# The causal mask moved from TensorE to VectorE in a fused Perceiver block

## What is computed

```python
x = x + fake_quant(layernorm(x)) @ fake_quant(ctx)          # cross step, 16 x 1024 x 1024 context
h = layernorm(x)
q, k, v = split(h @ qkv_w + qkv_b)                          # 32 heads of 32
q, k = rope(q), rope(k)
scores = einsum("bqhd,bkhd->bhqk", q, k) / sqrt(32)
scores = scores + (1.0 - causal) * -66504.0                 # keys after the query are hidden
x = x + (softmax(scores) @ v) @ out_w + out_b
x = x + layernorm(x) @ W.T + bias + low-rank updates        # feed-forward step
```

## Time and profile before

| | us |
|---|---|
| median of 3 runs | 648.58 (647.05 to 649.16) |
| the profiled execution's own time | 650.46 |
| its span, first to last instruction | 648.8 |
| TensorE busy | 606.3 (93%) |
| VectorE busy | 447.7 (69%) |
| ScalarE busy | 297.8 (46%) |
| length of one pair in the loop | 59.53 |

### The profile page before, as it was taken

The page is one execution under the profiler, slowest core; times in us unless marked ns, Lnnn a source line. Parts: engine busy times, 40 slices in busy tenths (PEclk is TensorE's granted clock), DMA queues, the critical chain, the costliest instruction groups (busy, mean ns, idle before and its releaser), DMA issues.

```text
span 648.8 us, 12624 instructions
## 1 busy us (share of the span) xinstructions
PE 606.3 (93%) x4832; PEld 301.0 (46%) x4832; DVE 447.7 (69%) x895; ACT 297.8 (46%) x374; POOL 11.1 (2%) x20
## 2 busy tenths in 40 slices
PE   1659979998999999999999999999999999899997
PEld 0224434454545554554455455545544554345453
DVE  7599965877756863885487568737774569777661
ACT  5886865673465355555544653554331243101010
POOL 3000000000000000000000000000000000000000
PEclk9859999999899999999999999999999999899999
DMA  9999984871176136416631761364240052113221
GB/s 319 386 389 397 349 320 154 269 249 69 44 261 216 67 134 224 162 65 229 222 119 53 257 219 65 132 224 130 97 157 6 1 191 105 47 67 128 85 78 48
DMA packets 38494, 109.17 MB, mean 168 GB/s; under 512 B 4026, under 2 KB 4282, under 8 KB 38464
## 3 DMA queue, kind: packets, MB, share of 16 engines
q1 hardware_dynamic: 36688, 104.35, 45.7%
q0 software_dynamic: 1344, 4.23, 1.7%
q10 hardware_dynamic: 432, 0.18, 0.1%
HBM read 100.35 MB, written 8.39 MB: 168 GB/s over the span
## 4 chain that ended last, share of the span: by engine, by line
PE 82%; DVE 9%; DMA 3%; SPq 2%; issue 2%; ACT 1%; DVEq 0%; ACTq 0%
PE dense L1084 17%; PE dense L1085 16%; PE dense L1086 16%; PE cross L1116 7%; PE turn L1075 7%; PE dense L1210 4%; PE dense L1212 4%; PE dense L1211 4%; PE score L1173 2%; SPq L534 2%; DMA wq<-in_ctx 2%; PE score L1197 2%; DVE wq L753 1%; DMA lnt<-in_ctx 1%; PE dense L1097 1%
## 5 line engine op out<-in xcount | busy, mean ns | idle before, releaser
L1084 PE MATMUL dense<-wq,xn_h 128*128 128x512 f16 x448 | 172.4, 385 | 4.8 <-DVE at L785 2.3
L1085 PE MATMUL dense<-wq,xn_h 128*128 128x512 f16 x448 | 171.8, 384 | 0.0
L1086 PE MATMUL dense<-wq,xn_l 128*128 128x512 f16 x448 | 171.6, 383 | 0.0
L309 ACT ACTIVATE code<-raw,cst,qc 128x1024 uint8<-128x1024 f32 x77 | 93.8, 1236 | 11.2 <-DMA raw<-in_ctx 10.8
L1116 PE MATMUL cross<-code,q1t 128*128 128x512 f16 x256 | 75.2, 400 | 5.6 <-DVE xa L760 3.1
L1086 PEld LDWEIGHTS dense<-wq,xn_l 128*128 128x128 f16 x448 | 44.3, 99 | 54.3 <-issue 2.5
L1084 PEld LDWEIGHTS dense<-wq,xn_h 128*128 128x128 f16 x448 | 44.2, 99 | 53.8 <-issue 8.9
L1085 PEld LDWEIGHTS dense<-wq,xn_h 128*128 128x128 f16 x448 | 44.3, 99 | 42.2 <-issue 1.9
L309 ACT ACTIVATE code<-lnt,cst,qc 128x1024 uint8<-128x1024 f32 x35 | 43.3, 1238 | 27.5 <-DMA lnt<-in_ctx 20.6
L782 DVE TENSOR_REDUCE smx<-score 128x8 f32<-128x512 f32 x32 | 21.9, 685 | 43.9 <-PE score L1173 43.8
L325 ACT ACTIVATE at<-turn 128x512 f32<-128x512 f32 x32 | 19.0, 595 | 71.9 <-PE turn L1075 71.9
(11 more groups left out here) (146 smaller groups left out, 845.5 us busy)
## 6 DMA issues: line engine op xcount, KB each, us to landing
raw<-in_ctx SPq DMA_DIRECT2D x77, 512.0 KB, 4.7
lnt<-in_ctx SPq DMA_DIRECT2D x35, 512.0 KB, 4.3
wq<-in_qkv_w SPq DMA_DIRECT2D x13, 512.0 KB, 11.8
wo<-in_ctx SPq DMA_DIRECT2D x8, 512.0 KB, 8.6
wq<-in_ctx SPq DMA_DIRECT2D x8, 512.0 KB, 11.5
wo<-in_qkv_w SPq DMA_DIRECT2D x8, 512.0 KB, 12.8
x_scratch<-xb SPq DMA_DIRECT2D x8, 512.0 KB, 3.0
wq<-x_scratch SPq DMA_DIRECT2D x8, 512.0 KB, 3.6
```

The costliest lines, as they stand in the source:

```text
L309: act.activation(low_bytes, src, ACT.Identity, scale=qc[:, 1:2], bias=z2).then_inc(s_u8, 1)
L1084: pe.matmul(bank[:, :], a_h[:, k, :], w_hi, start=(k == 0 and not started), stop=False)
L1085: pe.matmul(bank[:, :], a_h[:, k, :], w_lo, start=False, stop=False)
L1086: ins = pe.matmul(bank[:, :], a_l[:, k, :], w_hi, start=False, stop=(k == KC - 1 and not last))
```

## The change

From pair 1 on (`masked_by_vector`), TensorE makes no mask products, and each score product starts and ends its own accumulation. `softmax_in` begins with one new VectorE instruction that adds 51 times the mask to the bank and writes the sum to `pr`, and the reduction and the subtraction then read `pr`. The wait on `s_pt` stands before that new instruction, and a new semaphore `s_msk` takes the place of `s_sub` where TensorE waits for a bank of `S`. Besides, the first turn of probabilities moves: `p_turn(i,0)` from k-step 6 of block 3 to k-step 0 of block 4, and `p_turn(i,1)` from k-step 7 of block 3 to k-step 2 of block 4, with the wait `turned(i,2)` in front of the first.

```diff
+        s_msk = sem("s_msk")
+        def masked_by_vector(i):
+            return not isinstance(i, int) or i > 0
...
                 dve.wait_ge(s_sc, 4 * i + g + 1)
+                if masked_by_vector(i):
+                    dve.wait_ge(s_pt, 4 * i + g - 1)
+                    dve.scalar_tensor_tensor(p3, mask_rows, MASK_SEL, s3, ALU.mult, ALU.add).then_inc(s_msk, 1)
+                    dve.wait_ge(s_msk, 4 * i + g - 3)
+                    s3 = p3
                 link(dve.tensor_reduce(smx[:, g % 2, :], s3, AX.X, ALU.max))
-                if above(4 * i + g - 1):
+                if above(4 * i + g - 1) and not masked_by_vector(i):
                     dve.wait_ge(s_pt, 4 * i + g - 1)
                 dve.tensor_tensor(p3, s3, smx[:, g % 2, :].unsqueeze(2).to_broadcast([P, HPG, SEQ]),
                                   ALU.subtract).then_inc(s_sub, 1)
...
+            def read_by_softmax(i, count):
+                if masked_by_vector(i):
+                    pe.wait_ge(s_msk, 4 * i - 4 + count)
+                else:
+                    pe.wait_ge(s_sub, 4 * i + count)
...
                 if half:
-                    pe.wait_ge(s_sub, 4 * i + 2)
+                    read_by_softmax(i, 2)
                 elif above(4 * i):
                     pe.wait_ge(s_cl, 4 * i)
-                for n in range(2):
-                    rows = slice(n * SEQ, (n + 1) * SEQ)
-                    pe.matmul(S[n][:, :], row_of[rows, :], mask_rows[rows, :, :], start=True, stop=False)
+                vector = masked_by_vector(i)
+                if not vector:
+                    for n in range(2):
+                        rows = slice(n * SEQ, (n + 1) * SEQ)
+                        pe.matmul(S[n][:, :], row_of[rows, :], mask_rows[rows, :, :], start=True, stop=False)
...
-                                            qkt[rows, 2 * half + 1, c:c + SEQ], start=False, stop=(m == 3 and b == 1))
+                                            qkt[rows, 2 * half + 1, c:c + SEQ], start=vector, stop=vector or (m == 3 and b == 1))
...
-                    pe.wait_ge(s_sub, 4 * i + 4)
+                    read_by_softmax(i, 4)
...
-                qkv(i, 3, {1: [at(c, 7)], 2: [at(m, 2)], 5: [at(turned, i, 0), at(qk_turn, i, 2)], 6: [at(turned, i, 2), at(p_turn, i, 0)], 7: [at(p_turn, i, 1)]})
-                qkv(i, 4, {1: [at(m, 3)], 4: [at(evacuated, i, 1), at(qk_turn, i, 3)], 6: [at(c, 8)], 7: [at(c, 9)]})
+                qkv(i, 3, {1: [at(c, 7)], 2: [at(m, 2)], 5: [at(turned, i, 0), at(qk_turn, i, 2)], })
+                qkv(i, 4, {0: [at(turned, i, 2), at(p_turn, i, 0)], 1: [at(m, 3)], 2: [at(p_turn, i, 1)], 4: [at(evacuated, i, 1), at(qk_turn, i, 3)], 6: [at(c, 8)], 7: [at(c, 9)]})
```

## The result

| | before | after |
|---|---|---|
| median, us | 649.04 (7 runs) | 653.34 (7 runs) |
| ratio after to before | | 1.0062, 95% interval 1.0042 to 1.0083 |
| span of the profiled execution, us | 648.8 | 652.8 |
| TensorE / VectorE busy, us | 606.3 / 447.7 | 602.9 / 466.2 |
| length of a loop pair, us | 59.53 | 59.82 |

The change costs 0.62%, 4.3 us, where 1.6 us had been forecast. TensorE is busy 3.4 us less, and the kernel is slower.

A forecast was written before the change was run, and what follows sets the result against it. TensorE bounds the loop now; after the change VectorE's chain from first scores to `x_turn` would. Pair 1 +0.94, pairs 2 to 5 +0.92, pair 6 +0.05, pair 7 -0.3: +1.6 us on 648.58, so 650.2, range 645.5 to 653.5.

The forecast's parts named there:

- TensorE's saving of 0.89 us a pair: Loop pair: 0.64 us from dropping the mask products and 0.25 from moving the turn, were VectorE never late.
- the stalls forecast at 0.5 and 0.6: Loop pair: new TensorE waits, 0.5 us at `qk_turn(i,2)` for its rotation and some 0.6 at `x_turn` for `lnt`.
- +0.23: Pairs 2 to 5: `x_turn` comes 0.23 us later, so each pair gets longer by that; +0.92 over four pairs.
- Pair 6: No `row_stats` there; two added instructions make it 0.39 us late, against 0.34 saved before: +0.05.
- pair 7: Room at its softmax saves time, but the projection stalls 0.5 us behind the later `c_low(7,0)`: -0.3.
- Pair 1: Already bound by VectorE; later weight step, row statistics and second softmax, then two more instructions, delay the turn: +0.94.
- A, the cheaper step: Rival: the added VectorE instruction costs 0.60 us instead of 0.73, giving 647.1 us; chance 0.12.
- The two rules of the Trainium skill: PSUM sources cost 62 cycles more than SBUF (0.5 us a pair won back); semaphores between chained instructions cost nothing (price 0.60).
- B, the cover: Rival: VectorE's chain does not bind and only TensorE's saving is left, giving 643.5 us; chance 0.08.
- C, the clock in the loop: Rival: new stalls at `x_turn` or `qk_turn` lower the clock in pairs 2 to 6, 1.4 us each: 657.2; chance 0.06.
- D, stalls in a row: Rival: room at `c_low(i,1)` and `qk_turn` goes wrong, 0.3 to 0.5 us more a pair: 652.6 us; chance 0.12.
- the case for 650.2 itself: Main case: +1.6 us on the median 648.58, own range 648.9 to 651.5; chance 0.62.

The follow-up runs named there:

- two of the reordered kernels: Changed kernel with third rotation between first softmax steps, chunk 8 later; one also without row statistics (648.07 us), one with the mask half on VectorE (650.10 us).

## Why the prediction was right where it was, and what it missed

**The bound was right.** The prediction held that the stretch from the first scores to the write of `lnt` has 1.96 us of slack on VectorE and would be given 2.92 us. The stretch to `x_turn` was forecast at 34.38 us and measured at 34.38, with some luck in the last digit: VectorE's chain is 33.06 instead of 33.10, the hand-over to TensorE 0.13 instead of 0.09. The added step was put at 0.73 us and takes 0.72. TensorE's saving of 0.89 us a pair was right by the kernel without a mask (59.53 - 58.62 = 0.91), and the stalls forecast at 0.5 and 0.6 are 0.50 and 0.51.

**The loop was 0.06 short.** +0.23 was forecast and +0.29 measured. The `x_turn` comes when it was said to. But it then holds TensorE for 297.56 - 296.63 = 0.93 us instead of 0.87. The timeline of its weight loads fits that: before, the first one starts at 292.95, 0.22 us ahead of the turn and covered by a running product; now it starts at 296.62, 0.01 ahead of the turn. Four such pairs make 0.24; pair 2 has 0.1 more, which isn't explained. Pair 6 was put at +0.05 and is +0.12, pair 7 with all behind it at -0.3 and is -0.16. The 0.34 us that the prediction sets against the lateness in pair 6 have no working in it. The stall in pair 7, put at 0.5 though 525.23 - 524.82 is 0.41, is 0.52: the projection starts at 529.63 and could have at 529.11.

**Pair 1 was mis-sized, by a wait that the prediction did not list.** It said "then +0.38 of stall at `qk_turn(1,3)`: the last weight step, the row statistics and the second softmax come 0.73 later". They come 1.45 later, as the distance from the start of the scores to the second softmax went from 159.13 - 135.82 = 23.31 to 161.76 - 137.00 = 24.76. The 0.7 us between are the wait of chunk 8 for `cross_evac`: TensorE could have begun it at 152.90 and begins at 153.56, while before it began at 150.92 with nothing to wait for. `cross_evac` lies behind both late softmax steps and a rotation on VectorE. In the loop the same wait is 0.07 us. In pair 1, chunk 8 gates quantisation 14, and that the last weight. That this path binds is shown by the kernel with `w(31)` before `q(14)`, which gets 2.94 us of pair 1 back. The sum for pair 1 was +0.94 and is +1.62. The prediction followed the late softmax to the turns and to the second softmax, and left out the evacuation that stands between them and its reader. The other half, the chain behind the second softmax, was right: 1.45 + 1.46 = 2.91 us later `lnt`, measured 2.90.

**What the sum cannot give.** By the profiled executions, the change is worth 2.8 us, while the medians say 4.3, with an interval of 2.7 to 5.4. In 67 runs of the kernel before, the time goes with the mean granted clock: 30 with 0.984 have a mean of 648.3 us, 11 with 0.981 one of 649.3, six with 0.976 one of 650.1. The seven runs of the changed kernel have a mean clock of 0.979, the 67 of before 0.982; by the slope of those 67 runs, 0.30 us for 0.001, an estimate of 1.1 us. It is consistent with a slow stretch of the clock that comes more often, and where it comes was not seen: in the profiled execution the loop has a clock of 1.00, and slow stretches lie in much the same places as before.

**The rivals.** A, the cheaper step: out, 0.72. The two rules of the Trainium skill that the prediction set beside it (the page "VectorE: DVE Perf Modes", sections "The TRN2 errata" and "The DRAIN you can't avoid") don't agree with these rows either: the reductions take 686 ns from SBUF and 685 from PSUM, with no 62 cycles between them, and a step whose successor waits for it takes 0.72 us against 0.61 for one without. B, the cover: out. C, the clock in the loop: out, 1.00 in every pair; its 1.4 us a stall was not worked out, as its own rows give up to 1.7. D, stalls in a row: not in the changed kernel, where `c_low` kept its room, but its mechanism, "a ScalarE step pushed behind a quantisation", is just what spoilt two of the reordered kernels by 0.43 us a pair. The chance given to slower by over 0.3% was 0.40, the case for 650.2 itself 0.62. The measured 653.34 lies in the stated range, but only 0.16 us below its upper end, and outside the case's own range of 648.9 to 651.5. That end was set by rival D, which did not come true, so it is partly luck that the range held. Of the 3.1 us above 650.2, some 0.5 are the kernel before, whose median rose from 648.58 to 649.04; 1.2 are the sum, which gave 1.6 instead of 2.8, most of it by chunk 8 in pair 1 and the refill of 0.06 a pair; 1.1 are the estimate for the clock; the rest is open.

## What to carry to other kernels

Before work is moved from a full engine to one that is 69% busy, read where the idle 31% lie: sum the second engine's work over the stretch that it must finish between two meetings with the first. Here 1.96 us were free in that stretch of a pair, and 2.92 were put in; half of it (1.46) fitted and gave a pair of 58.95 us once the order of steps on VectorE, TensorE and ScalarE was mended. When a step is made late or reordered, list everything that waits for each of its followers, on the third engine too.

## What had not been expected of the hardware

A stall that ends in fp32 transposes cost 0.06 us more than its length: the group of eight takes 0.93 us instead of 0.87, and the next product starts 0.49 us after a group of four (269.67 to 270.16) instead of 0.43 (272.11 to 272.54).

Removing a wait of 2.3 us in pair 1 gave more than its length: 647.97 - 643.72 = 4.2 us for the kernel with the turns moved, by medians of two sessions, and 38.12 - 34.29 = 3.8 us from the scores to the turn of pair 1 in the profiled executions. Behind that wait the mean granted clock had been 0.72 over six microseconds, as in the kernel before, and with the wait gone it is 1.00 there. In the changed kernel the same mending gave 2.8 us, as there VectorE and not TensorE set the end of pair 1: TensorE still waits for `lnt` there.
